# GCN layers of a graph kernel: own rows accumulated into the scanned PSUM bank, scales masked off segment ends

## What is computed

```python
deg = segment_sum(ones_like(dst), dst)        # dst holds a self loop per node too
dis = rsqrt(where(deg > 0, deg, 1.0))
norm = dis[src] * dis[dst]
h = x @ W_in + b_in
for i in range(3):
    xw = h @ Ws[i]
    msg = xw[src] * norm[:, None]
    agg = segment_sum(msg, dst) + bs[i]
    h = relu(agg)
# and around it: x = layernorm(x + h)
```

## Time and profile before

| | |
|---|---|
| median of 3 runs | 4212.16 us (4201.67 to 4219.30) |
| the profiled execution | 4234.81 us |
| its span, first to last instruction | 4233.1 us |
| mean granted TensorE clock | 0.768 |
| busy: VectorE (DVE) | 3385.3 us, 80% |
| busy: TensorE (PE) | 2727.4 us, 64% |
| busy: ScalarE (ACT) | 2542.3 us, 60% |
| busy: GpSimd (POOL) | 2439.2 us, 58% |
| DMA | 644.05 MB, mean 152 GB/s |

### The profile page before, as it was taken

The page is one execution under the profiler, slowest core; times in us unless marked ns, Lnnn a source line. Parts: engine busy times, 40 slices in busy tenths (PEclk is TensorE's granted clock), DMA queues, the critical chain, the costliest instruction groups (busy, mean ns, idle before and its releaser), DMA issues. The chain is left out here.

```text
span 4233.1 us, 48032 instructions
## 1 busy us (share of the span) xinstructions
PE 2727.4 (64%) x11826; PEld 1768.2 (42%) x11826; DVE 3385.3 (80%) x7569; ACT 2542.3 (60%) x5535; POOL 2439.2 (58%) x2202
## 2 busy tenths in 40 slices
PE   2777877888870588845444553442888787577774
PEld 1555555555550244425433442341444444244442
DVE  2688999999997788837765774883999999699886
ACT  1677777778872366635553562442777777465554
POOL 5455555566630566436636646755566662587777
PEclk7999899999995677756766765565899999566555
DMA  3377567566652888727765764662233332333332
GB/s 87 120 176 182 172 188 193 178 201 193 194 181 74 236 254 254 224 90 225 237 202 167 235 215 140 196 193 74 66 85 85 85 85 60 87 97 97 94 95 68
DMA packets 402066, 644.05 MB, mean 152 GB/s; under 512 B 127455, under 2 KB 207720, under 8 KB 401790
## 3 DMA queue, kind: packets, MB, share of 16 engines
q1 hardware_dynamic: 332030, 527.96, 41.0%
q0 software_dynamic: 69760, 113.02, 11.0%
HBM read 347.78 MB, written 296.81 MB: 152 GB/s over the span
## 5 line engine op out<-in xcount | busy, mean ns | idle before, releaser
L1603 POOL DMA_INDIRECT gs_g<-table_xw,slot_idx x588 | 614.6, 1045 | 454.4 <-issue 250.1
L896 POOL DMA_INDIRECT gs_t<-table_x,slot_idx x392 | 435.1, 1110 | 370.1 <-POOLq L83 144.4
L505 POOL DMA_INDIRECT gs<-x,src_idx x200 | 215.9, 1079 | 406.4 <-DMA xd_rows<-gd 319.6
L378 PE MATMUL ps<-ident,own_g 128*128 128x128 f32 x588 | 145.8, 395 | 466.5 <-DVE own_g L1705 383.3
L1649 ACT ACTIVATE hT_g<-u_g 128x512 f32<-128x512 f32 x147 | 92.5, 630 | 516.5 <-DVE u_g L1717 340.9
L1710 DVE TENSOR_TENSOR_SCAN agg_g<-same_seg,agg_g,ps 128x512 f32<-128x512 uint8 x147 | 187.8, 1278 | 228.7 <-DMA table_x<-x_b 104.3
L1272 POOL DMA_INDIRECT slot_idx<-node_map,src_idx x200 | 239.5, 1198 | 196.6 <-DMA slot_idx<-node_map,src_idx 92.9
L378 PEld LDWEIGHTS ps<-ident,own_g 128*128 128x128 f32 x588 | 97.9, 200 | 507.3 <-DVE own_g L1705 415.9
L505 POOL DMA_INDIRECT gd<-x,dst_idx x200 | 245.2, 1226 | 60.9 <-issue 60.3
L1879 POOL DMA_INDIRECT out<-x_t,end_idx x196 | 232.8, 1188 | 65.0 <-issue 58.8
L896 POOL DMA_INDIRECT own_t<-table_x,own_idx x196 | 225.6, 1151 | 59.7 <-issue 59.7
(11 more groups left out here) (366 smaller groups left out, 9479.7 us busy)
## 6 DMA issues: line engine op xcount, KB each, us to landing
table_xw<-xw_b SPq DMA_DIRECT2D x147, 512.0 KB
table_x<-x_b SPq DMA_DIRECT2D x98, 512.0 KB
own_g<-table_xw SPq DMA_DIRECT2D x147, 256.0 KB
x_in<-x SPq DMA_DIRECT2D x49, 512.0 KB
y_g<-table_x SPq DMA_DIRECT2D x49, 512.0 KB
table_xw<-xw_g SPq DMA_DIRECT2D x98, 256.0 KB
out<-y_g SPq DMA_DIRECT2D x49, 512.0 KB
pen_t<-pen_row SPq DMA_DIRECT2D x98, 256.0 KB
```

Source lines behind the costliest of these rows:

```text
L378: last = nc.tensor.transpose(to[0:width, j * P:(j + 1) * P], t[:, j * width:(j + 1) * width], ident[:])
L505: pool.indirect_dma_start(out=to[k % 3][:, j * D:(j + 1) * D], out_offset=None, in_=x, in_offset=bass.IndirectOffsetOnAxis(ap=of[:, n:n + ...
L896: pool.indirect_dma_start(out=self.B[L % RING][g][:, t * D:(t + 1) * D], out_offset=None, in_=table, in_offset=bass.IndirectOffsetOnAxis(a ...
L1603: pool.indirect_dma_start(out=gs[c % 6][:, j * D:(j + 1) * D], out_offset=None, in_=tables[layer], in_offset=bass.IndirectOffsetOnAxis(ap= ...
```

## The change

Segment stage: a new tile `end4` is loaded from `nxt_row` (one where the next slot belongs to the same segment), turned into 1 at a segment's last slot and 0 elsewhere, and multiplied into `dis4` and `root4`. `inv4`, the square of `dis4`, is nought there too. Rows that no segment ends on are thus written as zeros, and the own rows can be added before the scan and not behind it: they stand at a segment's end, and count once.

Graph layers: the own rows are multiplied with the identity into the bank that the scan reads (`start` set on the first of the four), the gathered rows are accumulated into the same bank, and `T_O`, `u` and L1717 are gone. `T_X` has four banks and `agg` four buffers; relu reads `agg` directly. TensorE now takes the own rows first and the gathered ones after them. VectorE does the own bias of chunks 0 and 1 ahead of the loop and of chunk t+2 in round t, behind scan t. Node tiles are 21, 21 and 7 in the layers (before 25, 24, 0), in every second round, in the last layer in every fifth; attribute chunks come in rounds 0, 2, 5, 7, 10 and so on (before 1, 4, 7 ...). The lines for SyncE's own loads and table stores are not touched.

```diff
--- before.py
+++ after.py
@@ -999,6 +999,7 @@
         one = tile("one")
         number = tmp.enter_context(nc.sbuf_tensor("number", [P, W], I32))
         own = tile("own")
+        end4 = tile("end4", TILES)
         own_rows = tmp.enter_context(nc.sbuf_tensor("own_rows", [TILES // 2, 2, P], F32))
         pre_row, suf_row, penP_row, penQ_row = (tile(n, P, 1) for n in ("pre_row", "suf_row", "penP_row", "penQ_row"))
         carry_rows = [tile(f"carry_row{k}", P + 1, 1) for k in range(6)]
@@ -1020,6 +1021,7 @@
                     sp.dma_start(cont[h * SECT:(h + 1) * SECT, :], sections(nst_row)).then_inc(S("masks_in"), 16)
                     sp.dma_start(nxt[h * SECT:(h + 1) * SECT, :], sections(nxt_row)).then_inc(S("masks_in"), 16)
                 sp.dma_start(z[:], sections(z8[0:4, :])).then_inc(S("z_in"), 16)
+                sp.dma_start(end4.rearrange("p (c j) -> p c j", j=SUB), nxt_row.rearrange("o (c p j) -> p c (o j)", p=P, j=SUB)).then_inc(S("nxt4_in"), 16)
                 sp.dma_start(zs[:], sections(z8[4:8, :])).then_inc(S("zs_in"), 16)
                 sp.wait_ge(S("cnt_fix"), 1)
                 sp.dma_start(sections(cnt_row), cnt[0:SECT, :]).then_inc(S("cnt_out"), 16)
@@ -1179,7 +1181,13 @@
                 V.tensor_tensor(zs[:], zs[:], run[:], ALU.mult).then_inc(S("a_self"), 1)
                 v.wait_ge(S("root4"), 1)
                 V.reciprocal(dis4[:], root4[:]).then_inc(S("dis4"), 1)
+                v.wait_ge(S("nxt4_in"), 16)
+                V.tensor_scalar(end4[:], end4[:], -1.0, 1.0, ALU.mult, ALU.add).then_inc(S("end4"), 1)
                 v.wait_ge(S("dis4"), 1)
+                v.wait_ge(S("end4"), 1)
+                V.tensor_tensor(dis4[:], dis4[:], end4[:], ALU.mult).then_inc(S("dis_end"), 1)
+                V.tensor_tensor(root4[:], root4[:], end4[:], ALU.mult).then_inc(S("root_end"), 1)
+                v.wait_ge(S("dis_end"), 1)
                 V.tensor_tensor(inv4[:], dis4[:], dis4[:], ALU.mult)
                 v.wait_ge(S("own_ps"), 2)
                 V.tensor_scalar(own_idx[:], ps[:, 6, 0:TILES], float(NT + GT - 1), None, ALU.min)
@@ -1506,18 +1514,19 @@
             def ring(name, n, width=CH):
                 return [tmp.enter_context(nc.sbuf_tensor(f"{name}_g{layer}_{k}", [P, width], F32)) for k in range(n)]
 
-            gs, own, agg, u, hT = (ring(n, k) for n, k in (("gs", 6), ("own", 4), ("agg", 3), ("u", 2), ("hT", 3)))
+            gs, own, agg, hT = (ring(n, k) for n, k in (("gs", 6), ("own", 4), ("agg", 4), ("hT", 3)))
             xw, v_b, x2_e = (ring(n, 3) for n in ("xw", "v_b", "x2_e"))
             x1_e = ring("x1_e", 8)
             st, sd, rs, nm = (ring(n, 3, k) for n, k in (("st", 12), ("sd", 4), ("rs", 4), ("nm", 4)))
-            T_X, T_O, T_W = (ps[:, 0, :], ps[:, 1, :]), (ps[:, 2, :], ps[:, 3, :]), (ps[:, 4, :], ps[:, 5, :])
+            T_X, T_W = [ps[:, k, :] for k in range(4)], (ps[:, 4, :], ps[:, 5, :])
 
             def live(c):
                 return 0 <= c < G_CH
 
             y = [tmp.enter_context(nc.sbuf_tensor(f"y_g{layer}_{k}", [P, 2 * CH], F32)) for k in range(5)]
             y_st, y_sd, y_rs, y_nm = (ring(n, 3, k) for n, k in (("y_st", 24), ("y_sd", 8), ("y_rs", 8), ("y_nm", 8)))
-            N_Y = (N_CH + 1 - layer) // 2 if layer < 2 else 0
+            Y_FIRST, Y_STEP = (0, 21, 42)[layer], (2, 2, 5)[layer]
+            N_Y = min(N_CH, (21, 42, N_CH)[layer]) - Y_FIRST
 
             ea_in = [tmp.enter_context(nc.sbuf_tensor(f"ea_in_g{layer}_{k}", [P, SUB, 96], F32)) for k in range(3)]
             ea_t = [tmp.enter_context(nc.sbuf_tensor(f"ea_t_g{layer}_{k}", [96, CH], F32)) for k in range(2)]
@@ -1526,7 +1535,8 @@
 
             def ea_chunk(t):
 
-                return t // 3 if t % 3 == 1 and 0 <= t // 3 < N_E else None
+                k = (2 * t + 1) // 5
+                return k if t >= 0 and t == 5 * k // 2 and k < N_E else None
 
             def ea_rows(attr, k):
                 c = 3 * k + layer
@@ -1534,10 +1544,10 @@
 
             def node_chunk(t):
 
-                return t // 2 if t % 2 == 0 and 0 <= t // 2 < N_Y else None
+                return t // Y_STEP if t % Y_STEP == 0 and 0 <= t // Y_STEP < N_Y else None
 
             def of_all(k):
-                return (layer * ((N_CH + 1) // 2)) + k
+                return Y_FIRST + k
 
             def edge_rows(table, c, base=NT):
                 return table[base + c * CH:base + (c + 1) * CH, :].rearrange("(p j) f -> p (j f)", p=P)
@@ -1610,14 +1620,19 @@
                 def _(pe):
                     for t in range(G_CH + 3):
                         if live(t):
-                            if t >= 2:
-                                pe.wait_ge(S("agg"), t - 1)
+                            if t >= 4:
+                                pe.wait_ge(S("agg"), t - 3)
+                            pe.wait_ge(S("own_bias"), SUB * (t + 1))
+                            by_part = T_X[t % 4].rearrange("f (p j) -> f j p", j=SUB)
+                            for j in range(SUB):
+                                last = nc.tensor.matmul(by_part[:, j, :], own[t % 4][:, j * D:(j + 1) * D], ident[:],
+                                                        start=j == 0, stop=False, skip_group_check=True)
+                            last.then_inc(S("own_ps"), 1)
                             pe.wait_ge(pool_dma[f"gcn{t % 6}"], gather_count(t))
-                            turn(pe, T_X[t % 2], gs[t % 6]).then_inc(S("xsT_ps"), 1)
-                            pe.wait_ge(S("own_bias"), SUB * (t + 1))
-                            if t >= 2:
-                                pe.wait_ge(S("with_self"), t - 1)
-                            turn(pe, T_O[t % 2], own[t % 4]).then_inc(S("own_ps"), 1)
+                            for j in range(SUB):
+                                last = nc.tensor.matmul(T_X[t % 4][:, j * P:(j + 1) * P], gs[t % 6][:, j * D:(j + 1) * D], ident[:],
+                                                        start=False, stop=j == SUB - 1, skip_group_check=True)
+                            last.then_inc(S("xsT_ps"), 1)
                         k = ea_chunk(t - 2)
                         if k is not None:
                             pe.wait_ge(S(f"ea_in{k % 3}"), 32 * (k // 3 + 1))
@@ -1643,10 +1658,10 @@
                     for t in range(G_CH + 8):
                         c = t - 1
                         if live(c):
-                            act.wait_ge(S("with_self"), c + 1)
+                            act.wait_ge(S("agg"), c + 1)
                             if c >= 3:
                                 act.wait_ge(S("h_ps" if last_layer else "xw_ps"), c - 2)
-                            nc.scalar.activation(hT[c % 3][:], u[c % 2][:], ACT.Relu).then_inc(S("hT"), 1)
+                            nc.scalar.activation(rows4(hT[c % 3][:]), agg[c % 4].rearrange("f (p j) -> f j p", j=SUB), ACT.Relu).then_inc(S("hT"), 1)
                         c = t - 3
                         if live(c) and not last_layer:
                             act.wait_ge(S("xw_ps"), c + 1)
@@ -1694,27 +1709,29 @@
                 @block.vector
                 def _(v):
                     V = nc.vector
-                    V.memset(agg[2][:], 0.0).then_inc(S("no_sums"), 1)
+
+                    def own_bias(c):
+                        landed(v, "own_in", 4, c)
+                        for j in range(SUB):
+                            k = c * SUB + j
+                            blk = own[c % 4][:, j * D:(j + 1) * D]
+                            V.scalar_tensor_tensor(out=blk, in0=bs_row[layer][:], scalar=root4[:, k:k + 1], in1=blk,
+                                                   op0=ALU.mult, op1=ALU.add).then_inc(S("own_bias"), 1)
+
+                    V.memset(agg[3][:], 0.0).then_inc(S("no_sums"), 1)
+                    own_bias(0)
+                    own_bias(1)
                     v.wait_ge(S("no_sums"), 1)
                     for t in range(G_CH + 7):
                         if live(t):
-                            landed(v, "own_in", 4, t)
-                            for j in range(SUB):
-                                k = t * SUB + j
-                                blk = own[t % 4][:, j * D:(j + 1) * D]
-                                V.scalar_tensor_tensor(out=blk, in0=bs_row[layer][:], scalar=root4[:, k:k + 1], in1=blk,
-                                                       op0=ALU.mult, op1=ALU.add).then_inc(S("own_bias"), 1)
                             v.wait_ge(S("xsT_ps"), t + 1)
                             if t:
                                 v.wait_ge(S("agg"), t)
-                            V.tensor_tensor_scan(agg[t % 3][:], same_seg[:, t * CH:(t + 1) * CH], T_X[t % 2], agg[(t - 1) % 3][:, CH - 1:CH], ALU.mult, ALU.add).then_inc(S("agg"), 1)
-                        c = t - 1
-                        if live(c):
-                            v.wait_ge(S("own_ps"), c + 1)
-                            v.wait_ge(S("agg"), c + 1)
```

(8 more changed lines are left out.)

## The result

The changed kernel takes 4370.3 us, median of four runs (4369.01 to 4380.57), against 4213.15 before: a ratio of 1.0389 (95% interval 1.0359 to 1.0420), slower by 157 us. The ratios in this text and the quotients of the medians (here 1.0373) differ by up to 0.2%. Forecast were 4348 us in a range of 4237 to 4412. Its profiled execution took 4380.57 us with a span of 4378.8.

A forecast was written before the change was run, and what follows sets the result against it. No engine was full; the layers ran at the gathers' pace plus waits, and the change would close rings through a load's latency. Last layer 120, layers 0 and 1 14, rest 2: +136 us, giving 4348 us, range 4237 to 4412.

The forecast's parts named there:

- Each sign that it named: Graph layers: VectorE idle before L1718, scans 8.7 us apart in last layer, 13.6 us pairs, 1.9 us products, no L1717.
- the ring: Graph layers: VectorE's wait for own rows precedes work leading to the store and next load, so turns cost load latency; 0.75.
- +120: Last layer: 38 rounds of 8.74 us, two quick ones and six node tiles make 357 us instead of 237.
- +14: Layers 0 and 1: each +7 us, from pairs +30, last four chunks -7 and a shorter layer end -16.
- +2: Segment stage: three added VectorE operations, 1.1 us, and a load in 16-byte pieces, 1 us.
- 2.23: Last layer: us from VectorE's `nm` of chunk T-8, through `x2` and the store, to the load of T.
- L: Latency of the 256 KB own-row load: 4.2 us taken in layers 0 and 1, 3.7 in the last layer.
- the term from `y_sd` to the store: Layers 0 and 1: from ScalarE's `y_sd` to the table store's issue, 4.94 us of each 13.6 us pair.
- the stride: Layers 0 and 1: `hT` now reads `agg` with a stride, priced at 0.4 us, nothing at the low end.
- D: Rival: the standstill at each layer's start goes, 75 us over three layers, rings stay: +61, 4273 us; chance 0.14.
- B: Rival: TensorE becomes the bound, plain fp32 products taking 4.4 us for four blocks: 4796 us; chance 0.05.
- C: Rival: the ring doesn't close, own rows land in time and gathers set a 5.20 us pace: 4083 us; chance 0.06.

The follow-up runs named there:

- open versions: Changed kernel with own rows' load two chunks ahead, own bias last in the round, or own bias one chunk ahead, among others: 4151.94, 4170.24, 4209.17 us.
- the step alone: Kernel before with only the own bias of chunk t+2 taken in round t: 4458.4 us (1.1319) on one chip, 4648.14 us (1.1063) on another.

## Why the prediction was right

**The mechanism.** Each sign that it named is there: VectorE waits before L1718 for own rows, 449.3 us in 87 places; own products take 1.06 to 2.05 us where nothing interrupts them, 1.92 in the median; 9.5 us lie between the last scan and the next layer. Opening the ring in three ways, each in one place, took the whole loss away, and closing it in the kernel before, with nothing else of the change, brought it back and more.

**The sum.** Forecast were +120, +14 and +2. The profiles show +114.2, +47.8 and +0.4, 162.4 together, and the medians +157. The term that decides and the mechanism were right. That +136 came within 22 us is no proof of each part, since layers 0 and 1 cost over three times what was forecast for them, inside a range that was wide enough for it. The difference of the two profiled executions, 145.8 us, is nearer to 136 than the layers are, but only because the unchanged dense stage happened to end 23.4 us earlier.

**Last layer, +120 forecast.** Chunks 8 to 48 took 3003.08 - 2650.14 = 352.9 us where 357 were forecast and 237.4 stood: +115.5. Its terms: 2.23 measured 2.24; L of 3.7 measured 3.48; own bias to `nm` with its share of the tiles 3.23 measured 3.28. The whole layer is +114.2. By the Trainium skill's page "DMA: Bandwidth & Descriptors", section "Anatomy of one DMA — SWDGE (gpsimd) path", whose fit is for transfers of the GpSimd path, L would be 2.6 us, an estimate. The trace has more at every load of this layer, all of them issued by SyncE: 2.65 us at the first and 2.76 at the lowest of chunks 8 to 45.

```profile
2650.14 1.27 DVE L1732 TENSOR_TENSOR_SCAN agg_g<-same_seg,agg_g,ps 128x512 f32<-128x512 uint8 x1
...
3003.08 1.28 DVE L1732 TENSOR_TENSOR_SCAN agg_g<-same_seg,agg_g,ps 128x512 f32<-128x512 uint8 x1 [1.15 <-PE ps L1633]
```

**Layers 0 and 1, +14 forecast, +47.8 measured.** This is the sum's largest miss. The pairs were forecast at 13.6 us and took 271.8 / 19 = 14.3, so +38.5 and +36.6 instead of +30. L was right (4.32 and 4.33 in the mean of the pairs' waited loads, for 4.2). What was short is mainly the term from `y_sd` to the store: 4.94 and 0.4 for the stride, 5.34 together, where the pairs have 5.81 and 5.85 in the mean. In the 40 pairs of the two layers behind the first it is 5.54 to 5.57 us in 27, and 6.03 to 7.05 in the 13 where two attribute loads and the store of the turned attributes are issued by SyncE ahead of the table store (above: `xw` done at 2078.59, the store issued at 2079.62). The working let the attribute chunks cost nothing because it looked at ScalarE, and didn't count their issues on SyncE, which stand in the ring. The stride itself was about right: relu takes 1113 ns instead of 630, 0.48 for 0.4. The last four chunks gave 4.4 and 3.0 for 7, the shorter tail 16.8 and 13.1 for 16 (layer 1's tail was shorter to begin with). The rest, 5 us a layer, came in the first chunks, which the working left as they were: the standstill there is still present (in layer 0 VectorE is idle for 18.0 us before one scan and 9.8 before the next, for 24.9 before) and the first chunks as a whole took longer, not less.

**Segment stage, +2 forecast.** From its first load to layer 0's, 520.5 us against 520.1. This stretch takes 514.8 to 526.6 us in the profiles of this text, so +2 can be neither shown nor refused. Two of the three operations are as priced, the first is shorter:

```profile
1358.67 0.20 DVE L1185 TENSOR_SCALAR end<-end 128x200 f32<-128x200 f32 x1
1358.97 0.37 DVE L1188 TENSOR_TENSOR dis<-dis,end 128x200 f32<-128x200 f32 x1
1359.25 0.36 DVE L1189 TENSOR_TENSOR root<-root,end 128x200 f32<-128x200 f32 x1
```

**The rivals.** D fell: up to the scan of chunk 6 layers 0 and 1 took 5 us longer, the last layer 3 less, where 25 less were its price. B fell: products of fp32 with plain operands took 1.06 to 2.05 us per four blocks, not 4.4; that is under twice the 0.66 and 1.11 us of four transposes in the kernel before. C, the faster side, asked for own rows that land in time; the load two chunks ahead makes it true, and gives 4152 and not 4083, for C took the gathers' 5.20 us as the pace. All open versions and the kernel before run at 5.9 to 6.25 us a chunk. The 5.20 come from one gather of 1.00 us; with the longer ones in it the mean is higher. In layer 0 of the version with the load ahead 206.0 us lie between the first gather of chunk 10 and that of chunk 44: 151.0 in gathers, 39.7 between them with nothing waited for, 15.3 waiting. That is 5.6 us a chunk of their own in a pace of 6.06, so they are near the bound and aren't shown to be it. C's price was too low by this, and the forecast's reading of the pace was too; neither has a part in its sum.

## What to carry to other kernels

When an operation is taken earlier on an in-order engine, follow its data backwards through every queue to what stands ahead of it there, and ask whether that in turn waits for something behind the moved operation; if so, the round costs the whole chain, latency included, however idle the engines are. Move the load by as many rounds as the use. A long wait cost little here at the end of a round and was paid in full ahead of what feeds it, so the remedy may be a move of one line in either queue; and in such a ring every issue on a queue has a price, those of unrelated transfers too.

## What was not expected

The open versions share one pace whatever their order: 5.91 to 6.25 us a chunk, with TensorE's doubled products or without, and with own biases one or two ahead. In the slow rounds of the version with the load ahead TensorE gets through its instructions a few at a time, with 0.3 to 1.8 us between, and none of its releasers is named:

```profile
1970.61 1.06 PE L1633 MATMUL ps<-ident,own_g 128*128 128x128 f32 x2 [1.02 <-issue]
...
1972.72 0.60 PE L1633 MATMUL ps<-ident,own_g 128*128 128x128 f32 x2 [1.04 <-issue]
...
1974.14 0.37 PE L1633 MATMUL ps<-ident,own_g 128*128 128x128 f32 x1 [0.83 <-issue]
...
1974.85 0.78 PE L1633 MATMUL ps<-ident,own_g 128*128 128x128 f32 x2 [0.33 <-issue]
```

Sixteen more instructions a chunk moved the mid-layer pace by hardly anything (5.1 us over three layers, within the spread of the open versions), so this isn't shown to be the bound either, and what sets 6.1 us is open. The second surprise is the spread between chips: 4192 to 4213 us for the kernel before on four occasions, 3936 on another chip.

The two surprises meet in the traces. The kernel before with the step alone was profiled on the quick chip (4463.18 us) and on a usual one (4649.05). Of the 186 us between them 84 lie in the dense stage, which ended at 1221 instead of 1305 us, 67 between each layer's first load and its scan of chunk 6, and 54 in the attentions; chunks 6 to 44, where the rings set the pace, took 19 us more on the quick chip. And the idle time that is put down to "issue", in which an engine waited for nothing that the profile shows, is gone on the quick chip: TensorE's products, ScalarE and VectorE have 0.0, 0.2 and 0.6 us of it in the whole program, and 358.1, 270.7 and 72.6 us on the usual one (weight loads and GpSimd have it on both). All other profiles here have 290 to 458 us of it before products. ScalarE before `hT`, first on the quick chip, then on the usual one, where 127.0 us of the idle time are such:

```profile
L1649 ACT ACTIVATE hT_g<-u_g 128x512 f32<-128x512 f32 x147 | 92.8, 632 | 717.7 <-DVE u_g L1721 717.7
L1649 ACT ACTIVATE hT_g<-u_g 128x512 f32<-128x512 f32 x147 | 92.8, 631 | 775.2 <-DVE u_g L1721 648.2
```

The chips thus differ by these gaps, and the standstill at the start of the layers, 20.6 us before a scan of layer 0 on the usual chip and 4.3 at most on the quick one, goes with them. What makes the gaps, and why one chip has none, no run shows. The loss by the rings isn't made of them: the step alone costs 452 us on the usual chip and 523 on the quick one.
